# Filling the key stacks of two attention layers in four awaited steps

## What is computed

```python
# layer 0
q, k_self, v_self = split(_ln(x, g1, be1) @ w_qkv + b_qkv)
k_ctx, v_ctx = split(context @ w_ckv + b_ckv)
scores = einsum('bthd,bshd->bhts', q, concat(k_self, k_ctx)) * scale   # causal for the own keys
x = x + softmax(scores) @ concat(v_self, v_ctx)
x = x + (gelu(_ln(_ln(x, g2, be2), gf, bf) @ w1 + b1, approximate=False) @ w2 + b2)
# layer 1
Q = layer_norm(x) @ wq.T + bq;  K = context @ wk.T + bk;  V = context @ wv.T + bv
scores = where(key_mask == 0, NEG_INF, einsum('bqhd,bkhd->bhqk', Q, K) / sqrt(hd))
out = x + softmax(scores) @ V @ wo.T + bo
```

## Time and profile before

| | |
|---|---|
| median of 3 runs | 465.14 us (463.82 to 467.96) |
| the profiled execution | 466.13 us |
| its span, first to last instruction | 463.7 us |
| busy: PE / PEld / DVE / ACT / POOL | 384.7 / 278.6 / 295.5 / 262.5 / 139.8 us |
| mean granted TensorE clock | 0.915 |
| chain that ended last | PE 50%, DVE 18%, issue 9%, ACT 8%, DMA 8%, POOL 4% |
| SP waiting for a key fill at L369 | 37.1 us, 7 times, longest 6.2 |

### The profile page before, as it was taken

One profiled execution on the slowest core, in us unless ns is written; L12 is line 12 of the kernel. 1 busy time (PEld: TensorE's weight loads), 2 busy tenths in 40 slices (PEclk: granted clock), 3 DMA queues, 4 the chain that ended last, 5 costly groups with the idle time before them and its releaser, 6 DMA issues.

```text
span 463.7 us, 20194 instructions
## 1 busy us (share of the span) xinstructions
PE 384.7 (83%) x8885; PEld 278.6 (60%) x8885; DVE 295.5 (64%) x738; ACT 262.5 (57%) x459; POOL 139.8 (30%) x207
## 2 busy tenths in 40 slices
PE   3668879996989799988899798979898989686766
PEld 1346657564666576657576567667676676453654
DVE  5426786469568774796658675796389459706232
ACT  2567635763756476464846386556656756343451
POOL 7100533046205520363105520461047106302000
PEclk9957986999999899998999899998999999877586
DMA  6755164115342542153404542253201400121101
GB/s 192 198 151 123 54 171 140 34 56 137 108 119 93 121 147 59 69 129 111 134 3 146 106 131 60 94 122 122 60 26 43 125 3 26 58 82 47 48 4 45
DMA packets 41974, 42.86 MB, mean 92 GB/s; under 512 B 3208, under 2 KB 34392, under 8 KB 41888
## 3 DMA queue, kind: packets, MB, share of 16 engines
q1 hardware_dynamic: 40436, 39.86, 31.2%
q0 software_dynamic: 624, 1.26, 1.0%
q10 hardware_dynamic: 828, 0.46, 0.3%
HBM read 23.65 MB, written 17.83 MB: 89 GB/s over the span
## 4 chain that ended last, share of the span: by engine, by line
PE 50%; DVE 18%; issue 9%; ACT 8%; DMA 8%; POOL 4%; SPq 1%; ACTq 1%; DVEq 0%; POOLq 0%
PE dense L689 12%; PE dense L712 7%; DVE top L1011 5%; PE key L845 3%; PE mixed L875 3%; PE mixed L883 3%; DMA k_stack<-scratch_k 3%; PE key L836 3%; PE side L908 3%; PE dense L694 3%; PE dense L702 2%; PE query L795 2%; PE query L803 2%; DVE k_part L1001 2%; ACT probs L523 2%
## 5 line engine op out<-in xcount | busy, mean ns | idle before, releaser
L1011 DVE TENSOR_REDUCE top<-query 128x8 f32<-128x1024 f32 (+1 forms) x96 | 117.2, 1220 | 70.9 <-PE query L803 54.7
L523 ACT ACTIVATE probs<-key 128x1024 f32<-128x1024 f32 x96 | 98.4, 1025 | 81.9 <-PE key L845 55.7
L462 POOL TENSOR_TENSOR top<-top 128x8 bf16<-128x8 f32 (+1 forms) x96 | 20.3, 213 | 207.2 <-DVE top L1011 206.5
L845 PE MATMUL key<-top_row,spread 48*64 48x128 bf16 x1536 | 48.7, 226 | 3.8 <-ACT top_row L528 3.6
L455 POOL TENSOR_TENSOR rstd_x<-var_eps_x,half 128x4 f32<-128x4 f32 x24 | 24.5, 1020 | 71.6 <-DVE var_eps_x L973 71.6
L544 ACT COPY o_t<-mixed 128x256 f32<-128x256 f32 x96 | 35.3, 368 | 13.4 <-PE mixed L896 7.8
L875 PE MATMUL mixed<-probs,v 128*32 128x128 f32 x1024 | 41.7, 281 | 0.0
L836 PE MATMUL key<-q_stack,k_stack 48*64 48x128 f16 x1024 | 40.1, 221 | 0.0
L689 PE MATMUL dense<-normed_ft,w 128*128 128x512 f32 x64 | 34.2, 663 | 5.1 <-ACT normed_ft L564 5.1
L845 PEld LDWEIGHTS key<-top_row,spread 48*64 48x64 bf16 x1536 | 33.8, 109 | 6.1 <-ACT probs L523 4.9
L908 PE MATMUL side<-cst,o_t 128*128 128x128 f32 x192 | 34.1, 304 | 0.7 <-ACT mix_t L551 0.7
(11 more groups left out here) (120 smaller groups left out, 782.1 us busy)
## 6 DMA issues: line engine op xcount, KB each, us to landing
k_stack<-scratch_k SPq DMA_DIRECT2D x16, 384.0 KB, 6.2
q_stack<-scratch_q SPq DMA_DIRECT2D x64, 96.0 KB
scratch_k<-k_part SPq DMA_DIRECT2D x8, 512.0 KB, 2.8
scratch_k<-k_part SPq DMA_DIRECT2D x16, 256.0 KB, 2.6
scratch_q<-q_part SPq DMA_DIRECT2D x16, 256.0 KB, 2.7
k_stack<-scratch_k SPq DMA_DIRECT2D x16, 192.0 KB
x_in<-in_x SPq DMA_DIRECT2D x8, 256.0 KB, 3.2
scratch_q<-q_part SPq DMA_DIRECT2D x16, 128.0 KB, 2.4
```

Source lines behind the costliest of these rows:

```text
L523: nc.scalar.activation(probs[u.number % 2][:].rearrange("p h q -> p (h q)"), key[:].rearrange("p h x -> p (h x)"), ACT.Exp, scale=SCALE).t ...
L845: ins = nc.tensor.matmul(key[T * n:T * n + T, h, a * P:(a + 1) * P], spread[u.layer][rows, A2 * h + a, T * n:T * n + T], top_row[u.number ...
L1011: nc.vector.tensor_reduce(maxima, query[:].rearrange("p h x -> p (h x)").rearrange("p (a k) -> p a k", a=w), AX_X, ALU.max, negate=True).t ...
```

## The change

A key fill of both layers is cut by head pair: four steps, each with one DMA per half of the partitions. From chunk 1 on, each step but the first waits until all that the chunk's fill has issued so far has landed. The counts that others wait for follow from the larger number of DMAs (128 instead of 32 in layer 0, 144 instead of 48 in layer 1). The bytes are the same. Chunk 0's fills are cut, but not waited for between steps.

```diff
+FILLS = {"k": 32 * A2, "q": 64, "k1": 32 * A2 + 16, "q1": 64}
...
             def fill_keys(name, c, stack, first):
                 sp.wait_ge(s_store[name], 32 * (c + 1))
-                for h in range(HALVES):
-                    at = HR * h + first
-                    sp.dma_start(stack[at:at + ROWS], rows_of(name, h)).then_inc(s_fill[name], 16)
+                for a in range(A2):
+                    if a > 0 and c > 0:
+                        sp.wait_ge(s_fill[name], FILLS[name] * c + FILLS[name] - 32 * (A2 - a))
+                    for h in range(HALVES):
+                        at = HR * h + first
+                        sp.dma_start(stack[at:at + ROWS, a:a + 1], rows_of(name, h)[:, a:a + 1]).then_inc(s_fill[name], 16)
...
                     if c > 0:
-                        sp.wait_ge(s_fill["k"], 32 * (c + 1))
+                        sp.wait_ge(s_fill["k"], FILLS["k"] * (c + 1))
                     fill_queries("q", c, q_stack[c % 2], 0, c > 0)
...
                     if u.layer == 0:
-                        pe.wait_ge(s_fill["k"], 32 * (c + 1))
-                        pe.wait_ge(s_fill["q"], 64 * (c + 1))
+                        pe.wait_ge(s_fill["k"], FILLS["k"] * (c + 1))
+                        pe.wait_ge(s_fill["q"], FILLS["q"] * (c + 1))
```

More of the change, by code:

```diff
@@ L381, in _ @@
                     if c > 0:
-                        sp.wait_ge(s_fill["k"], 32 * c)
+                        sp.wait_ge(s_fill["k"], FILLS["k"] * c)
                     sp.wait_ge(s_high["k_ctx"], c + 1)
@@ L398, in _ @@
                     if c > 0:
-                        sp.wait_ge(s_fill["q"], 64 * c)
+                        sp.wait_ge(s_fill["q"], FILLS["q"] * c)
                     store_high("q", c, Q_HIGH, twice(q_part[:, 0]))
@@ L421, in _ @@
                     if c > 0:
-                        sp.wait_ge(s_fill["k1"], 48 * c)
+                        sp.wait_ge(s_fill["k1"], FILLS["k1"] * c)
                     if c >= 2:
@@ L432, in _ @@
                     if c > 0:
-                        sp.wait_ge(s_fill["q1"], 64 * c)
+                        sp.wait_ge(s_fill["q1"], FILLS["q1"] * c)
                     store_high("q1", c, Q_HIGH, twice(q1_part[:, 0]))
@@ L494, in _ @@
                         pool.wait_ge(s_read["k1"], c)
-                        pool.wait_ge(s_fill["k1"], 48 * c)
+                        pool.wait_ge(s_fill["k1"], FILLS["k1"] * c)
                     nc.gpsimd.tensor_scalar(keep[:], mask_in[:], 0, 0, ALU.is_equal, ALU.is_equal).then_inc(s_keep, 1)
@@ L782, in by_query @@
                     if u.layer == 0:
-                        pe.wait_ge(s_fill["k"], 32 * (c + 1))
-                        pe.wait_ge(s_fill["q"], 64 * (c + 1))
-                    else:
-                        pe.wait_ge(s_fill["k1"], 48 * (c + 1))
-                        pe.wait_ge(s_fill["q1"], 64 * (c + 1))
+                        pe.wait_ge(s_fill["k"], FILLS["k"] * (c + 1))
+                        pe.wait_ge(s_fill["q"], FILLS["q"] * (c + 1))
+                    else:
+                        pe.wait_ge(s_fill["k1"], FILLS["k1"] * (c + 1))
+                        pe.wait_ge(s_fill["q1"], FILLS["q1"] * (c + 1))
                         pe.wait_ge(s_mask_keys, 32)
```

## The result

The changed kernel took 483.42 us (median of 4 runs, 481.04 to 488.44), the kernel before, run beside it, 464.48: a ratio of 1.038, 95% interval 1.029 to 1.047. The profiled execution took 483.31 us. The change makes the kernel slower, as forecast, but by some 18 us where 6.9 were forecast, and outside the range.

The account below looks back on a forecast made before the run. It took TensorE running dry behind its own layer 0 key fill, and SP's serial list, as the bounds; 8.3 - 2.6 - 2.8 + 4.0 = +6.9 us gave 472.0 us against the median, range 462 to 480.

Parts of the forecast that it names:

- the stops: TensorE's unnamed halts behind layer 0's key fill, chunks 4 to 7, would go, giving 3.3 to 3.9 us, chunk 7 2.8.
- Rival B: TensorE's stops are not the key fill's doing and stay: +9.9 us, 475.0 us; chance 0.12.
- what is late next: Behind the longer fill, TensorE waits for the context in chunks 1, 3 to 6; VectorE longer for x about 51 us.
- spare 4.0 to 5.3 us: Time the context load could be late unfelt: 5.3 us in chunks 4 and 5, 4.0 in chunk 6.
- A step's price: Each awaited 192 KB step of layer 0's key fill takes 2.75 us, so 11.0 us per fill.
- upper end: Highest step price for layer 0's key fill: an instruction block ahead of every second step, 3.4 us.
- the forecast's own rule: SP's delay lands whole in chunks 1 and 3 (+8.3 us); in chunks 4 to 6 spare time absorbs it (-2.6).
- the clock: Half-speed TensorE after new load waits in the rounds of chunks 1, 3, 4, 5, 6: 5 x 0.8 = +4.0 us.
- rival C: Dear steps of 3.2 us through instruction blocks and slow issues, fill 12.8: +15.9 us, 481.0 us; chance 0.12.
- Layer 1's key fill ... Cost 0: Layer 1's steps, chunks 1 to 7, send the mask 12.5 us late, within 16 us spare: cost 0.
- Rival D: No low clock behind the new waits: +2.9 us, 468.0 us; chance 0.14.
- Rival A: Short steps in layer 0's key fill, 2.25 us each, fill 9.0: -5.5 us, 459.6 us; chance 0.12.

## Why the prediction was right and wrong

**Right: the stops.** They belong to layer 0's fill (they go with its steps and stay with layer 1's alone), and going they give 3.2 to 4.4 us a round by the account where the loads are out of the way; I had 2.8 to 3.9. Against that account's noise the agreement of the sizes is partly luck. Rival B falls.

**Right: what is late next.** VectorE waits for x and TensorE for the context, in the rounds named. In the rounds of chunks 1, 3 and 4 (timeline, in the form of the earlier trace rows):

```profile
51.84 0.88 DVE L973 BATCH_NORM_STATS2 stat_x<-x_in 128x6 f32<-128x128 f32 x4 [7.10 <-DMA x_in<-in_x]
...
138.84 1.11 PE L690 MATMUL dense<-cst,ctx_in 128*128 128x128 f32 x4 [3.84 <-DMA ctx_in<-in_ctx]
...
190.57 1.11 PE L690 MATMUL dense<-cst,ctx_in 128*128 128x128 f32 x4 [4.54 <-DMA ctx_in<-in_ctx]
```

The spare 4.0 to 5.3 us of the rounds of chunks 4 to 6 hold as well: two dummy loads fitted into them, three did not in the rounds of chunks 4 and 5. The round of chunk 2 cost -0.2 for a forecast of 0.

**Wrong: "A step's price", 2.75 us.** The step of the forecast that failed is the price that went into its sum, "I take 2.75, so 4 x 2.75 = 11.0 us per fill". The instruction blocks that a step meets were left to the upper end ("one ahead of every second step gives 2.75 + 0.65 = 3.4") and stand in the sum at nothing. Measured, a step took 3.0 us on average in the rounds of chunks 1 to 3 and 3.4 in those of chunks 4 to 7. The chain of waits over chunk 4's fill gives each step's landing (start us, us, what):

```profile
163.31 2.11 DMA k_stack<-scratch_k
...
165.79 2.80 DMA k_stack<-scratch_k
...
168.95 3.09 DMA k_stack<-scratch_k
...
172.41 3.36 DMA k_stack<-scratch_k
```

From one issue to the next the four took 2.6, 3.2, 3.5 and 3.7 us. The DMA queues say why. First a step of chunk 1 (39.7 to 41.4 us), then the fourth of chunk 4 (172.9 to 175.75); packets, MB, share of 16 engines:

```profile
q1 hardware_dynamic: 128, 0.20, 39.9%
```

```profile
q1 hardware_dynamic: 128, 0.20, 26.5%
q8 instruction: 1, 0.02, 2.1%
```

The same 128 packets, but with an instruction block of TensorE beside them. In the packet records that block runs from 173.70 to 174.64 on one engine; 93 key packets are through by 174.09, and the last three come after it, up to 175.29. The step waits for those. Of the 28 steps of the seven paced fills, 10 had no block beside them and took 2.62 us in the median (2.47 to 3.26); 18 had one and took 3.62. In the kernel with only layer 0 stepped it is 2.60 (11 steps) and 3.59 (17). Chunk 0's steps, which wait for nothing, are left out. So a step by itself was a little cheaper than my 2.75; what I mis-sized is how often it meets a block, and at what price. In the rounds of chunks 1 to 3, 5 steps of 12 did, about "every second"; in those of chunks 4 to 7, where a block moves every 3.5 to 4.2 us during the fill, 13 of 16 did.

The Trainium skill (DMA: Bandwidth & Descriptors, section Queues, rings and completion order) says that an engine takes turns between the queues it has work for, a packet at a time. After the change, the step shown looks like that: the block goes in among the key packets, and what lies behind it on its engine waits for that one packet. In the kernel before it did not: with 768 KB handed over at once, no block moved for 4.7 us, and the one that then moved started within 0.3 us of the start of the fill's last key packet (chunks 4 to 6) or 0.6 before it (chunk 7). It came 6.1 to 7.5 us after the block before it, against 3.5 to 4.2 after the change, so it was late and not merely unasked for. With two steps of 384 KB it again moved behind a half's packets or with the last of them, in the gap that the wait leaves. So the stops went by the gap, and whether a block also goes in among the packets seems to hang on how much has been handed over; why, no run here shows.

The Trainium skill (DMA: Bandwidth & Descriptors, section Anatomy of one DMA), which the prediction set beside its price, gives its 2.0 us plus bytes at 436 GB/s for DMAs that GpSimd issues; these are SP's. Its estimate of 2.45 us for 192 KB lay below the 2.62 us that a step without a block took here.

With the measured fills in place of mine, and the forecast's own rule: chunks 1 and 3 cost 5.2 + 4.6, chunks 4 to 6 cost (6.15 - 5.3) + (6.0 - 5.3) + (5.45 - 4.0) = 3.0, chunk 7 gives 2.8, the clock costs 4.0: +14.0. This term alone doubles the forecast, and rival C, which held it, was the nearest: 481.0 us, for which I gave 0.12. That its total came so near is luck in part, since it has neither the mask nor the dearer clock below. The fill is also not all of SP's delay: counted from the start of the fill, the context load went out 6.2, 7.1 and 3.4 us later than before in the rounds of chunks 4 to 6, where the fill alone was 6.15, 6.0 and 5.45 longer.

**Wrong: "Layer 1's key fill ... Cost 0".** GpSimd waited in chunk 7's round:

```profile
365.68 1.93 POOL L502 TENSOR_SCALAR keep<-mask_in 128x512 f32<-128x512 int32 x1 [5.28 <-DMA mask_in<-in_mask_BxS_ik]
```

I read the spare time in chunk 4's round, 16 us, and carried it to all. In chunk 7's round of the kernel before, the mask went out at 327.40 and was read at 344.06: 16.7 less 4.1 of flight (as measured after), so 12.6 us. After, it went out at 361.47, 34.1 later, while the units around it were 16.3 later: 17.8 us of delay of its own, where I had 12.5. Of this the layer 0 fill is 14.02 - 7.70 = 6.3, layer 1's 8.95 - 0.80 = 8.2, the rest the query fills and stores between. 17.8 - 12.6 = 5.2, and the account jumps by 5.2. This adds up to 19.2 us. In the whole it did not show as a gain when layer 1's steps went, since the rounds up to chunk 6 and the last units took it back. Why those rounds were dearer is not shown; the blocks fell into the steps in another way, which may be it.

**Mis-sized: the clock,** 0.8 us a wait. The windows of the low stretches behind the context waits of the rounds of chunks 4 and 5, columns as above:

```profile
189.75:196.58 6.83, 6.01 (x85) 5.10 (x86) 2.25 (x5) 2.62 (x5) 0.24 (x1) 0.50 0.32 100
240.95:251.19 10.24, 6.04 (x85) 5.13 (x86) 2.25 (x5) 2.97 (x7) 0.23 (x1) 0.50 0.35 104
```

The first is 6.8 us at half the clock and the second 10.2, where a stop of the kernel before was followed by 3.41; the transposes of the context take 1.11 us in place of 0.60. Behind the later fills the rounds of chunks 1, 3, 4 and 5 cost 7.2, 5.6, 2.4 and 3.5 us, and the delay of SP (less the spare time) accounts for 5.2, 4.6, 0.9 and 0.7. So 1.0 to 2.8 us per round is left for the clock and all else. Taking the lateness of the context load itself (6.2, 7.1, 3.4 us less the spare 5.3, 5.3, 4.0) for the rounds of chunks 4 to 6, which cost 2.4, 3.5 and 1.1, leaves a more even 1.5, 1.7 and 1.7. No run tells the clock's part of it from the rest. Rival D, no low clock, falls.

**Not foreseen: -3.1 us among the last units.** The kernel with only layer 1 stepped gives 2.7 at the same place, the one with only layer 0 stepped 1.0. The windows over TensorE's low stretch there, before and after, columns as above:

```profile
401.50:411.74 10.24, 8.15 (x20) 4.15 (x19) 2.25 (x11) 4.89 (x8) 1.02 (x1) 0.50 0.40 116
```

```profile
421.92:425.33 3.41, 3.25 (x14) 2.85 (x14) 2.21 (x13) 1.33 (x3) 1.02 (x1) 0.51 0.28 93
```

Before, half the clock lasts 10.2 us and reaches over a group of eight large matmuls (L689), which takes 6.39 us; after, it has ended and the same group (L695) takes 4.08: 2.3 of the 3.1 us. In all thirteen kernels the time between the two units around this place goes with this stretch: 29.1 us in the three where it lasts 3.4 us (the kernel after, only layer 1 stepped, two steps with loads ahead), 30.8 to 32.1 us in the ten where it lasts 10.2. Those three do not share either layer's steps, so this gain is not the steps' doing as far as the runs show; what decides the length of the stretch is open.

**The sum.** 14.0 by the forecast's rule with the measured fills (its 4.0 for the clock is in it), +5.2 by the mask, about +3 more than that 4.0 by the clock and the rest, -3.1 at the end, and small differences of the rounds of chunks 2 and 7: some 18 us. Since that "rest" is what remains of the account, the sum has to close; the steps and the mask are measured by themselves. Rival A needed steps below 2.47 us (2.40 by the prediction's own 2 us for each 0.1), and even steps free of blocks took 2.62.

What stays open is whether the cost of a step can be hidden by having two steps under way, each counted on a semaphore of its own. That wasn't tried.

## What to carry to other kernels

A large transfer cut into awaited pieces lets other queues' traffic through, instruction blocks among it, but it turns the issuing queue into a chain of round trips, and here each was as long as its last packets, on the one DMA engine that also carried a block, made it. Before you pace a transfer, list what stands behind it on that queue, round by round and down to the last round, and put the loads that are consumed soonest in front; here that order turned a loss of 3.8% into a gain of 1.6%. And cut as coarsely as the purpose allows: two pieces did the work of four.

## What the runs showed of the hardware

- One instruction block (16 KB, one packet on one engine) beside a 192 KB step lengthened it by 1.0 us: 3.62 against 2.62 us in the median. Steps of half the size (layer 1's, two DMAs of 48 KB) took 2.2 us where no block lay beside them, so half the bytes saved 0.4 us.
- Stops of TensorE of 2.0 to 3.1 us behind 768 KB handed over at once were gone with 384 KB at a time: the block moved in the gap between the two halves, 157.12 us in chunk 4's round.
- Waits of TensorE for the context of 3.8 to 6.1 us went with 6.8 to 10.2 us at half the clock; stops of 2.0 to 3.1 us with 3.4.
- Near the end of the program the same work took 29.1 us where a half-clock stretch lasted 3.4 us, and 30.8 to 32.1 us where it lasted 10.2.
